# Shared expert of a mixture-of-experts layer: gate, up and router with the tokens as the stationary operand

## The reference

```python
logits = x.astype(jnp.float32) @ router_w.T            # 64 experts, top 8
...
gu = x @ ws_gate_up                                     # 256 -> 2 * 192
sg, su = (gu[:, :SF], gu[:, SF:])
shared = jax.nn.silu(sg) * su @ ws_down                 # 192 -> 256
return routed + shared
```

## Time and profile before

| | us |
|---|---|
| median of 3 runs | 3035.03 (3033.9 to 3042.45) |
| the profiled execution's own time | 3023.01 |
| its span, first to last instruction | 3021.2 |
| PE / PEld busy | 2738.9 / 2297.6 |
| VectorE / ScalarE / GpSimd busy | 2202.1 / 1039.7 / 820.5 |
| mean granted TensorE clock | 0.955 |

### The profile page before, as it was taken

How to read it: one execution, slowest core, us unless ns; L and a number is a source line. 1 busy time by engine, 2 the same in 40 slices (tenths; PEclk the granted TensorE clock), 3 DMA queues, 4 the chain that set the end, 5 groups by cost and what they waited for, 6 DMA issues and landing times. The chain is left out here.

```text
span 3021.2 us, 61482 instructions
## 1 busy us (share of the span) xinstructions
PE 2738.9 (91%) x23816; PEld 2297.6 (76%) x23816; DVE 2202.1 (73%) x5944; ACT 1039.7 (34%) x1524; POOL 820.5 (27%) x858
## 2 busy tenths in 40 slices
PE   2599999999999999999999999999999999956886
PEld 1388888888888888888888888888888888736775
DVE  2467888887888887888888888888888888733332
ACT  1223433333334333333333333333333333211111
POOL 1000122222222222222222222222222222334334
PEclk7599999999999999999999999999999999967998
DMA  6633444443333333333333333333333331117785
GB/s 196 183 87 97 114 124 111 116 116 110 108 96 89 100 100 100 94 86 94 100 95 94 100 89 100 98 89 83 97 99 100 99 90 43 40 39 211 207 213 126
DMA packets 321183, 327.31 MB, mean 108 GB/s; under 512 B 45405, under 2 KB 302231, under 8 KB 320892
## 3 DMA queue, kind: packets, MB, share of 16 engines
q1 hardware_dynamic: 287100, 304.20, 35.6%
q0 software_dynamic: 33792, 19.17, 3.6%
HBM read 182.18 MB, written 212.37 MB: 131 GB/s over the span
## 5 line engine op out<-in xcount | busy, mean ns | idle before, releaser
L653 ACT ACTIVATE exps<-second 128x1024 f32<-128x1024 f32 x512 | 525.9, 1027 | 785.0 <-PE second L1135 777.1
L548 POOL DMA_INDIRECT expert_slots<-row_mem,sidx x512 | 509.1, 994 | 790.9 <-PE first L1117 553.8
L1215 PE MATMUL mixp<-w_h,r_part_h 128*128 128x256 f32 x3072 | 668.5, 299 | 40.1 <-DVE hid L906 24.0
L822 DVE TENSOR_REDUCE nm<-first 128x4 f32<-128x1024 f32 x512 | 623.2, 1217 | 93.1 <-PE first L1117 93.0
L1215 PE MATMUL mixp<-w_h,r_part_l 128*128 128x256 f32 x3072 | 609.7, 280 | 0.0
L1215 PE MATMUL mixp<-w_l,r_part_h 128*128 128x256 f32 x3072 | 609.3, 279 | 0.0
L1215 PEld LDWEIGHTS mixp<-w_h,r_part_h 128*128 128x128 f32 x3072 | 467.4, 189 | 97.0 <-DVE hid L906 31.7
L1215 PEld LDWEIGHTS mixp<-w_l,r_part_h 128*128 128x128 f32 x3072 | 468.4, 188 | 0.0
L1215 PEld LDWEIGHTS mixp<-w_h,r_part_l 128*128 128x128 f32 x3072 | 468.1, 188 | 0.0
L906 DVE SCALAR_TENSOR_TENSOR x_mem<-mixp,C,x_mem 128x256 f32<-128x256 f32 x768 | 329.6, 477 | 114.6 <-PE mixp L1215 114.2
L906 DVE SCALAR_TENSOR_TENSOR hid<-mixp,C,hid 128x256 f32<-128x256 f32 x704 | 300.7, 474 | 35.8 <-PE mixp L1215 33.8
(11 more groups left out here) (211 smaller groups left out, 3687.0 us busy)
## 6 DMA issues: line engine op xcount, KB each, us to landing
kst<-k_parts SPq DMA_DIRECT2D x256, 192.0 KB, 3.8
qst<-q_parts SPq DMA_DIRECT2D x256, 192.0 KB, 4.1
q_parts<-nat_h SPq DMA_DIRECT2D x128, 256.0 KB
k_parts<-ctx_part_h SPq DMA_DIRECT2D x64, 256.0 KB, 2.4
k_parts<-nat_h SPq DMA_DIRECT2D x64, 256.0 KB, 2.4
q_parts<-nat_l SPq DMA_DIRECT2D x64, 256.0 KB
exps<-in_wgu SPq DMA_DIRECT2D x39, 384.0 KB, 4.4
expert_slots<-row_mem SPq DMA_DIRECT2D x8, 1284.0 KB, 12.5
```

The source lines that it names most:

```text
L548: pool.e.indirect_dma_start(out=slots_dram, out_offset=bass.IndirectOffsetOnAxis(ap=sidx[b % 2][:, t, k:k + 1], axis=0), in_=row[b % 2][:, ...
L653: act.e.activation(exps[:, j % NU, :, :, :].rearrange("p k t s -> p (k t s)"), second[:, :, :].rearrange("p k s -> p (k s)"), ACT.Exp, sca ...
L822: dve.e.tensor_reduce(nm[u % 2][:, :, 2 * j:2 * j + 2].rearrange("p t k -> p k t"), first[:, :, :].rearrange("p k (t s) -> p k t s", t=TIL ...
L1215: m = pe.e.matmul(mixp[q % 2][:, t * D:(t + 1) * D], src[i][:, dt, t * P:(t + 1) * P], wmix[n][j][:, l, dt, :], start=(k == 0), stop=(k == ...
```

## The change

The router's weights are put in front of the shared expert's in one array wsgu (64 + 192 + 192 columns); rT and its load go. d_logits streams router and gate together (256 columns) with the tokens stationary, into misc; d_up, moved to place 143.52, two pieces behind d_logits (between them stands a mix piece), streams 192 columns into first. ScalarE does the tanh directly behind the exp of d_logits. VectorE multiplies in token layout at d_up's new place, and misc stays claimed until v_h1, the first of these operations. At 149.35, in the old place of gate, the new piece d_swap transposes the product (four transposes into misc), ScalarE copies it (a_sT), and misc stays claimed until then; h_turn is the next to claim it. The copy sT lies in the memory of xdT, so that the xdT copy now waits for the down product of the batch before.

```diff
-    "d_logits": 143.42, "d_top": 150.95, "d_pos": 156.45, "d_gate": 149.31, "d_up": 149.37, "d_down": 163.62,
+    "d_logits": 143.42, "d_top": 150.95, "d_pos": 156.45, "d_up": 143.52, "d_swap": 149.35, "d_down": 163.62,
...
-        rT = sb("rT", (P, DT, NE))
-        wsgu = sb("wsgu", (P, DT, 2 * FH))
+        wsgu = sb("wsgu", (P, DT, NE + 2 * FH))
...
-        sT_a = router_mem[0:FC, 1]
+        s_tok = router_mem[:, 1].rearrange("p a s -> p (a s)")[:, 0:TILES * FH].rearrange("p (t f) -> p t f", t=TILES)
+        sT = router_mem[0:FC, 0]
...
+        gates = misc[:, :].rearrange("p (t n) -> p t n", t=TILES)[:, :, NE:NE + FH]
...
# scalar_program
                     act.wait_ge(t_dt, b + 1)
-                    act.wait_ge(t_up, b)
+                    act.wait_ge(t_dn, b)
...
                     act.e.activation(prob[:, :, :], prob[:, :, :], ACT.Exp).then_inc(a_p, 1)
-                elif what == "d_gate":
-                    b, = a
-                    act.wait_ge(t_gate, b + 1)
-                    act.wait_ge(t_dn, b)
+                    act.wait_ge(t_lg, b + 1)
+                    act.wait_ge(t_sw, b)
                     act.wait_ge(v_w, CHUNKS)
-                    act.e.activation(sT_a[:, :, :], misc[0:FC, :].rearrange("p (f s) -> p f s", f=2), ACT.Tanh,
-                                     scale=0.5).then_inc(a_th, 1)
+                    act.e.activation(s_tok, gates, ACT.Tanh, scale=0.5).then_inc(a_th, 1)
+                elif what == "d_swap":
+                    b, = a
+                    act.wait_ge(t_sw, b + 1)
+                    act.e.copy(sT, misc[0:FC, :].rearrange("p (f s) -> p f s", f=2)).then_inc(a_sT, 1)
...
# vector_program, d_up
-                    dve.e.scalar_tensor_tensor(sT_a[:, :, :], sT_a[:, :, :], 1.0, gv, ALU.add, ALU.mult).then_inc(v_h1, 1)
+                    dve.e.scalar_tensor_tensor(s_tok, s_tok, 1.0, gates, ALU.add, ALU.mult).then_inc(v_h1, 1)
...
-                    dve.e.scalar_tensor_tensor(sT_a[:, :, :], sT_a[:, :, :], 0.5, uv, ALU.mult, ALU.mult).then_inc(v_h2, 1)
+                    dve.e.scalar_tensor_tensor(s_tok, s_tok, 0.5, up, ALU.mult, ALU.mult).then_inc(v_h2, 1)
...
# tensor_program
-                    claim("misc", (v_ld, b + 1))
+                    claim("misc", (v_ld, b + 1), (v_h1, b + 1))
...
-                            m = pe.e.matmul(misc[:, t * NE:(t + 1) * NE], xdT[:, dt, t * P:(t + 1) * P], rT[:, dt, :],
+                            m = pe.e.matmul(misc[:, t * (NE + FH):(t + 1) * (NE + FH)], xdT[:, dt, t * P:(t + 1) * P],
+                                            wsgu[:, dt, 0:NE + FH],
                                             start=(dt == 0), stop=(dt == DT - 1))
...
+                elif what == "d_up":
+                    b, = a
+                    claim("first", (v_h2, b + 1))
+                    for t in range(TILES):
+                        for dt in range(DT):
+                            m = pe.e.matmul(bank1[0][:, t * FH:(t + 1) * FH], xdT[:, dt, t * P:(t + 1) * P],
+                                            wsgu[:, dt, NE + FH:], start=(dt == 0), stop=(dt == DT - 1))
+                    m.then_inc(t_up, 1)
+                elif what == "d_swap":
+                    b, = a
+                    claim("misc", (a_sT, b + 1))
+                    pe.wait_ge(v_h2, b + 1)
                     for f in range(2):
...
+                        for t in range(TILES):
+                            m = pe.e.transpose(misc[0:FC, f * S + t * P:f * S + (t + 1) * P],
+                                               s_tok[:, t, f * FC:(f + 1) * FC], ident)
+                    m.then_inc(t_sw, 1)
                 elif what == "d_down":
                     b, = a
                     claim("misc", (v_xd, b + 1))
-                    pe.wait_ge(v_h2, b + 1)
+                    pe.wait_ge(a_sT, b + 1)
```

More of the change, by code:

```diff
@@ L112, in build @@
 def build(nc, x_in, ctx_in, ctxT_in, wqT_in, wkvT_in, woT_in, qk_cols_in, bv_cols_in, bo_in, pw_in, uT_in,
-          w1T_in, w2T_in, b2_in, rT_in, wgu_in, wd_in, wsgu_in, wsd_in, out_pad):
+          w1T_in, w2T_in, b2_in, wgu_in, wd_in, wsgu_in, wsd_in, out_pad):
     NB, S, D = x_in.shape
@@ L123, in build @@
     KR = 3
-    NE = rT_in.shape[2]
+    NE = wgu_in.shape[0]
     CAP = 128
@@ L256, in build @@
         exT = [t[:, i, :].rearrange("p (a t) -> p a t", a=DT) for t in xhat for i in range(2)]
-        ehid = [sT_a[:, :, i * P:(i + 1) * P] for i in range(2)]
+        ehid = [router_mem[0:FC, 1, :, i * P:(i + 1) * P] for i in range(2)]
         ey = [X[i // 2][:, i % 2, :] for i in range(NY)]
@@ L289, in build @@
         a_mT, a_e, a_out = (sem(f"act_{n}") for n in ("mT", "exp", "out"))
-        a_z, a_gelu, a_c3, a_p, a_th, a_silu = (
-            sem(f"act_{n}") for n in ("zexp", "gelu", "c3", "pexp", "tanh", "silu"))
+        a_z, a_gelu, a_c3, a_p, a_th, a_sT, a_silu = (
+            sem(f"act_{n}") for n in ("zexp", "gelu", "c3", "pexp", "tanh", "sT", "silu"))
         t_g, t_bo, t_kp, t_vp, t_qt, t_q, t_ot, t_o, t_rt, t_z, t_mix, t_c3, t_b2, t_ht = (
             sem(f"pe_{n}") for n in ("g", "bo", "k", "v", "qt", "q", "ot", "o", "rt", "z", "mix", "c3", "b2", "ht"))
-        t_dt, t_lg, t_pos, t_gate, t_up, t_dn, t_et, t_eg, t_ed = (
-            sem(f"pe_{n}") for n in ("dt", "logits", "pos", "gate", "up", "down", "e_turn", "e_gate", "e_down"))
+        t_dt, t_lg, t_pos, t_up, t_sw, t_dn, t_et, t_eg, t_ed = (
+            sem(f"pe_{n}") for n in ("dt", "logits", "pos", "up", "swap", "down", "e_turn", "e_gate", "e_down"))
         t_same, t_dup = sem("pe_same"), sem("pe_dup")
@@ L569, in scalar_program @@
             act.e.copy(identr[:, :], hid[:, 0, 0:P]).then_inc(a_id, 1)
-            act.wait_ge(c_w, 16 * 9)
+            act.wait_ge(c_w, 16 * 8)
             def split_hi(c):
@@ L914, in vector_program @@
                     b, = a
-                    lg = misc[:, 0:TILES * NE].rearrange("p (t n) -> p t n", t=TILES)
+                    lg = misc[:, :].rearrange("p (t n) -> p t n", t=TILES)[:, :, 0:NE]
                     dve.wait_ge(t_lg, b + 1)
@@ L977, in vector_program @@
                     b, = a
-                    gv = misc[0:FC, :].rearrange("p (f s) -> p f s", f=2)
-                    uv = bank1[0][0:FC, :].rearrange("p (f s) -> p f s", f=2)
+                    up = bank1[0][:, 0:TILES * FH].rearrange("p (t f) -> p t f", t=TILES)
                     dve.wait_ge(a_th, b + 1)
-                    dve.e.scalar_tensor_tensor(sT_a[:, :, :], sT_a[:, :, :], 1.0, gv, ALU.add, ALU.mult).then_inc(v_h1, 1)
+                    dve.e.scalar_tensor_tensor(s_tok, s_tok, 1.0, gates, ALU.add, ALU.mult).then_inc(v_h1, 1)
                     dve.wait_ge(v_h1, b + 1)
                     dve.wait_ge(t_up, b + 1)
-                    dve.e.scalar_tensor_tensor(sT_a[:, :, :], sT_a[:, :, :], 0.5, uv, ALU.mult, ALU.mult).then_inc(v_h2, 1)
+                    dve.e.scalar_tensor_tensor(s_tok, s_tok, 0.5, up, ALU.mult, ALU.mult).then_inc(v_h2, 1)
                 elif what == "d_down":
@@ L1053, in turn @@
                 m.then_inc(sem_, 1)
-            pe.wait_ge(c_w, 16 * 9)
+            pe.wait_ge(c_w, 16 * 8)
             for dt in range(DT):
@@ L1263, in tensor_program @@
                     m.then_inc(t_pos, 1)
-                elif what in ("d_gate", "d_up"):
+                elif what == "d_up":
                     b, = a
-                    up = what == "d_up"
-                    claim("first" if up else "misc", (v_h2, b + 1) if up else (v_h1, b + 1))
-                    pe.wait_ge(a_dt, b + 1)
-                    for f in range(2):
[L1270 to L1274, removed]
+                    claim("first", (v_h2, b + 1))
[8 more added lines that the diff above has]
+                    pe.wait_ge(v_h2, b + 1)
+                    for f in range(2):
+                        for t in range(TILES):
+                            m = pe.e.transpose(misc[0:FC, f * S + t * P:f * S + (t + 1) * P],
+                                               s_tok[:, t, f * FC:(f + 1) * FC], ident)
+                    m.then_inc(t_sw, 1)
                 elif what == "d_down":
@@ L1277, in tensor_program @@
                     claim("misc", (v_xd, b + 1))
-                    pe.wait_ge(v_h2, b + 1)
+                    pe.wait_ge(a_sT, b + 1)
                     for t in range(TILES):
                         for f in range(2):
-                            m = pe.e.matmul(misc[:, t * D:(t + 1) * D], sT_a[:, f, t * P:(t + 1) * P], wsd[:, f, :],
+                            m = pe.e.matmul(misc[:, t * D:(t + 1) * D], sT[:, f, t * P:(t + 1) * P], wsd[:, f, :],
                                             start=(f == 0), stop=(f == 1))
@@ L1380 @@
         "b2": a["L0_ffn_b2"],
-        "rT": split_rows(a["L1_ffn_router_w"].T),
         "wgu": expert_rows(np.stack([a["L1_ffn_w_gate"], a["L1_ffn_w_up"]], 1), P),
         "wd": expert_rows(a["L1_ffn_w_down"], fc),
-        "wsgu": split_rows(a["L1_ffn_ws_gate_up"]),
```

(1 more changed line is left out.)

4 lines of the change are left out of this document (2 added, 2 removed).

## The result

The changed kernel takes 3122.27 us (median of 6 runs, 3118.37 to 3125.31), the kernel before 3040.81 us in 6 runs of its own: 81 us more. The ratio of the two is recorded as 1.0279 (95% interval 1.0263 to 1.0295), which is 85 us on the 3035 us of the forecast. The profiled execution took 3118.37 us, its span is 3116.6 us. The forecast was 3185 us, range 3085 to 3225: direction and range hold, but the loss of 85 us is 57% of the 150 us forecast, and a range 140 us wide is easily hit.

What follows compares the result with a forecast made beforehand. TensorE was taken to set the pace in three quarters of the kernel; 30 blocks x (1.93 us order and waits + 3.08 us half clock) = 150 us on the 3035 us median gave 3185 us, range 3085 to 3225.

Steps and rivals of the forecast that it cites:

- The order part: From logits to h_turn: changed TensorE work plus new waits at q_proj and h_turn, +1.93 us per block.
- PE's own work: Per block on TensorE: logits +0.81, up +1.30, gate and up removed -3.53, d_swap +0.53, in all -0.89 us.
- The waits: TensorE waits +0.48 us at q_proj for VectorE's gate operation and 2.34 us at h_turn for ScalarE's copy, per block.
- The clock part: Behind the h_turn wait, TensorE's clock falls to half in most blocks: +3.08 us per block (0 to 4.6).
- I take two such stretches per block: Behind h_turn, thin pieces keep half clock for two stretches of 1.54 us cost each, +3.08 us per block.
- One stretch: Rival: the mixture's dense products fall in the first half-clock stretch, so only one per block; 3139 us, chance 0.22.
- No additional fall: Rival: the clock does not fall more often, the waits alone cost 58 us; 3093 us, chance 0.14.
- Faster: Rival: both waits gone, TensorE's smaller work decides, 30 x -0.89 us; 3008 us, chance 0.09.
- SP's load: In the first microseconds: one load fewer, while TensorE waits for weights anyway; 0 to -1 us.
- GpSimd's queue: Keeps its order; its scatters wait for d_pos, which moves with TensorE; counted at nothing.
- the tile first: Held until v_h2, the next score piece comes 1 us later, so that cover makes it cost nothing.
- xdT's copy: Now waits for the previous batch's down product, 19 places of a 40-place block earlier; counted at nothing.

Runs made afterwards that it cites:

- fill: The changed kernel with 20 dense TensorE products per block put between d_swap and h_turn, result unused: 3091.33 us, ratio 1.0193 to the kernel before.
- early: The kernel before, old form of the products, with only gate and up moved to directly behind d_logits: 3120.94 us, ratio 1.0285 to the kernel before.
- v5: The changed kernel, tanh before exp, first gate operation earlier, up, h_turn, d_swap, d_top and score pieces reordered: 3048.43 us, ratio 1.0045 to the kernel before.
- fill10: The changed kernel with 10 dense TensorE products per block put between d_swap and h_turn: 3079.11 us, ratio 1.0140 to the kernel before.
- v1: The changed kernel, tanh before exp, first gate operation earlier, up back in its old place, q_proj and d_swap later: 3085.98 us, ratio 1.0169 to the kernel before.
- v3: The changed kernel, tanh before exp, first gate operation earlier, av and up before a score piece, d_swap behind out_turn: 3103.34 us, ratio 1.0226 to the kernel before.

## Why the prediction was right, and where it was off

**The order part, +1.93 us per block forecast, +1.88 measured** from logits to h_turn, and 1.89 by the fill. Its terms were less exact than their sum. The logits took 1.64 us plus 0.11 that the next piece's first products lost (1469.70 - 1469.28 = 0.42, commonly 0.31 behind logits before), +0.83 in all against +0.81 forecast. Up: 1.46 (forecast 1.30, which left out how the group starts). d_swap: 1481.82 - 1481.17 = 0.65 (0.53). PE's own work thus fell by 3.53 - 0.83 - 1.46 - 0.65 = 0.59 us, not by 0.89. The waits were 0.22 instead of 0.48, since VectorE was ready some 0.15 us earlier and PE came 0.2 us later, the up product being longer, and 2.16 instead of 2.34, because ScalarE's copy began at 1483.35, 0.10 us before the exp's end, where the forecast put it 0.05 behind: together 2.38 instead of 2.82. The waits were 0.44 too high and the work saved 0.30 too high; that these nearly cancel is luck. (2.38 - 0.59 is 1.79; the other 0.09 of the 1.88 lies in the pieces between.) What hid the ScalarE chain before, gate and up, was named rightly, and "early" shows it without the rest of the change. The drain of about 1380 ns that the Trainium skill, "ScalarE: Activation LUTs", What ACT_TABLE_LOAD costs, gives behind the load was again not there: load at 1481.14, exp at 1482.43.

**The clock part, +3.08 us per block forecast, +1.52 measured.** This is the mis-sized step. That the clock would fall in most blocks was right; it fell in all 27. The step that failed is "And it will not end as soon ... I take two such stretches per block, 2 x 1.54". In 17 of the 27 blocks it was one stretch of 3.4 us, beginning 6.0 to 7.2 us behind the gelu's table load, where h_turn stands at 5.8. Those blocks are 82.2 to 82.6 us long, some 1.3 us more than fill's, as one fall of the kernel before cost 1.54. The score pieces, the 32 narrow products and what followed were enough to bring full clock back, which I had judged too thin. In 5 blocks the stretch was 10.2 us long and began 2.0 to 2.2 us behind the load, before the wait; there the block is 83.6 to 83.7 us long, 2.5 us more than in fill: part of the half clock runs while PE stands still anyway and costs nothing. The other 5 blocks had 6.8 us, the length forecast: four of them, begun before the wait too, are 0.9 to 1.2 us longer than fill's, and the fifth, begun only 0.4 us before h_turn, 2.4 us. That a wait swallows part of the half clock is the second thing that the step left out. So it was the price more than the length that was wrong: half clock held for 5.3 us per block on average, against 6.8 forecast, and cost 1.52 us, against 3.08. With one stretch per block the sum would have been 3139, with the measured term 3035 + 30 x (1.88 + 1.52) = 3137; the measured ratio gives 3120 on that base. Of the remaining 17 us, 7 lie outside the steady blocks, as the profiled executions already differ by 95 and not 102 us. The others lie between the profiled executions and the ratio of the runs: the profiled execution before is 12 us under its median of 3035.03, that of the changed kernel only 4 us. The range held although the largest term was twice too high, because it reached down to 50 us of loss.

**The rivals.** "One stretch" (0.22) came nearest. "No additional fall" is what fill made real: forecast 3093, measured 3091. "Faster" needed both waits gone; v5 comes near to that and still does not gain the 27 us: the work saved in the changed kernel is 0.59 us per block and not 0.89, and small waits return. That SP's load, GpSimd's queue, the tile first and xdT's copy cost nothing held: none of them is in the list of waits.

## What to carry to other kernels

When work is moved out of a place where the bounding engine seemed merely busy, ask which chain on another engine it covered, and lay that chain against what is left: here the copy let h_turn start 2.84 us after the table load began (1483.98 - 1481.14), and PE had work for 0.68 us of that (1481.82 - 1481.14). A wait can cost a second time, by the clock, if its surroundings are thin, and a cheap test tells the two apart: fill the wait with products whose result nobody reads. Before a new form of a computation is blamed, move the old form to the same places.

## What the runs showed of the hardware

- More work on TensorE made the kernel faster: 20 products of 256 columns per block, 31 us less, 18 transposes of 128x128, 38 us less, 10 products, 43 us less. The interval of the 20 (1.0167 to 1.0218) lies above that of the 10 (1.0119 to 1.0160), but they ran on different chips, and the blocks are equally long in all three, 81.1 to 81.2 us.
- How long TensorE waited before a thin stretch went with how often the granted clock fell from 1.00 to 0.50 (2.4 and 1.2 GHz) at its end: 0.9 to 1.0 us, no fall in 24 blocks (fill10); 1.3 us, 17 falls in 28 blocks (v1); 1.7 us, 20 in 27 (v3) and 24 in 24 (early); 2.16 us, 18 in 18 (the change). Falls that came earlier in their block are left out. The pieces around the wait are not the same in these kernels, and v3 and early differ at equal waits, so the wait alone is not shown to be the cause.
- The clock also fell with no long wait before it: in 3 blocks of the kernel before, in 9 of the changed one and in 20 without gelu, each time 2.5 to 5.8 us ahead of h_turn, about where an idle of 0.55 us behind the 17-column products ends.
- The same length of half clock had different prices: 3.4 us behind the wait cost 1.3 us, 6.8 us begun just before h_turn 2.4 us, 6.8 us begun before the wait 0.9 to 1.2 us, and 10.2 us begun before the wait 2.5 us. TensorE standing still in it fits the difference: the wait shrank from 2.16 to 1.1 to 1.4 us in those blocks.
